# A four-way attention and feed-forward pair in float32: the short key blocks of the causal layer are put together in twos

## The reference, cut to what matters

```
x = x + attn_a(layernorm(x));  x = x + ffn(layernorm(x))
x = x + attn_b(layernorm(x));  x = x + ffn(layernorm(x))      # attn_b: causal

# attn_b, 16 heads of width 8
logits = einsum('bshd,bkhd->bhsk', q, k) / sqrt(8)
logits = where(k_pos > q_pos, -inf, logits)
attn   = softmax(logits, axis=-1)
out    = einsum('bhsk,bkhd->bshd', attn, v) @ W_out + b_out
```

## Time and profile before

| | |
|---|---|
| the profiled execution | 1573.21 us, span 1571.4 us |
| median of 3 runs | 1576.52 us |
| TensorE matmul busy | 1438.6 us, 92% |
| VectorE busy | 1235.9 us, 79% |
| ScalarE busy | 980.0 us, 62% |
| exponentials, L559 | 896, 794.2 us busy |
| job matmuls, L995 | 1792, 657.0 us busy |
| maxima, L785 | 1280, 815.2 us busy |
| weighted sums, L1045 | 3584, 441.6 us busy |
| chain that ended last | PE 70%, DVE 18%, ACT 5%, issue 4% |

### The profile page before, as it was taken

How to read it: one execution, slowest core, us unless ns; L and a number is a source line. 1 busy time by engine, 2 the same in 40 slices (tenths; PEclk the granted TensorE clock), 3 DMA queues, 4 the chain that set the end, 5 groups by cost and what they waited for, 6 DMA issues and landing times.

```text
span 1571.4 us, 26128 instructions
## 1 busy us (share of the span) xinstructions
PE 1438.6 (92%) x9625; PEld 701.7 (45%) x9625; DVE 1235.9 (79%) x3106; ACT 980.0 (62%) x1259; POOL 108.9 (7%) x210
## 2 busy tenths in 40 slices
PE   3699999999999999999988988999999999999888
PEld 2444344434444443444436654444444444444455
DVE  7589999999999998999937757787787877777254
ACT  4427777777777777777774432666666666666622
POOL 6020000000000000000001112000000000000010
PEclk9859999999999999999999985999999999999999
DMA  3720111111101111110001323111121112210000
GB/s 95 221 57 7 27 28 29 29 29 28 28 6 25 28 28 29 28 28 2 2 1 54 83 79 76 35 29 29 29 53 32 29 29 47 38 29 2 8 21 27
DMA packets 40055, 58.39 MB, mean 37 GB/s; under 512 B 7796, under 2 KB 19448, under 8 KB 39928
## 3 DMA queue, kind: packets, MB, share of 16 engines
q1 hardware_dynamic: 39928, 56.72, 15.2%
HBM read 36.77 MB, written 18.87 MB: 35 GB/s over the span
## 4 chain that ended last, share of the span: by engine, by line
PE 70%; DVE 18%; ACT 5%; issue 4%; DMA 2%; SPq 1%; POOL 0%; DVEq 0%; ACTq 0%; POOLq 0%
PE psum L995 25%; PE psum L1045 23%; DVE maxima L785 11%; PE psum L1009 6%; PE psum L1142 5%; PE psum L938 4%; ACT probs L559 3%; DVE junk L782 3%; PE psum L1147 2%; PE psum L1017 1%; PE psum L948 1%; DVE xn L706 1%; PE psum L1062 1%; DMA k_parts<-parts 1%; DMA qop<-shift_rows 1%
## 5 line engine op out<-in xcount | busy, mean ns | idle before, releaser
L559 ACT ACTIVATE probs<-psum 128x1024 f32<-128x1024 f32 (+3 forms) x896 | 794.2, 932 | 300.4 <-PE psum L1009 192.7
L785 DVE TENSOR_REDUCE maxima<-psum 128x1 f32<-128x512 f32 x1280 | 815.2, 684 | 72.8 <-PE psum L995 67.8
L995 PE MATMUL psum<-kop,qop 62*128 62x512 f32 (+3 forms) x1792 | 657.0, 465 | 56.5 <-DVE maxima L782 20.0
L1009 PE MATMUL psum<-qop,kop 64*128 64x512 f32 (+3 forms) x1792 | 498.2, 411 | 10.4 <-ACT probs L559 7.8
L995 PEld LDWEIGHTS psum<-kop,qop 62*128 62x128 f32 x1792 | 289.6, 191 | 487.6 <-DVE maxima L785 325.4
L1045 PE MATMUL psum<-probs,vwin 128*32 128x512 f32 (+3 forms) x3584 | 441.6, 565 | 3.9 <-ACT probs L559 2.0
L782 DVE CUSTOM_DVE_ANT_0 junk<-psum,mask 128x384 bf16<-128x384 f32 (+3 forms) x512 | 237.4, 487 | 75.3 <-PE psum L995 69.8
L1009 PEld LDWEIGHTS psum<-qop,kop 64*128 64x128 f32 x1792 | 242.0, 189 | 55.7 <-ACT probs L559 44.7
L1045 PEld LDWEIGHTS psum<-probs,vwin 128*32 128x32 f32 x3584 | 71.8, 109 | 105.5 <-issue 84.6
L1017 PE MATMUL psum<-half_ident,key_mask 64*128 64x64 bf16 x1024 | 92.7, 198 | 0.0
L1142 PE MATMUL psum<-ffn_xt,wffn 128*128 128x512 f32 x192 | 87.6, 594 | 0.0
(11 more groups left out here) (88 smaller groups left out, 709.9 us busy)
## 6 DMA issues: line engine op xcount, KB each, us to landing
qop<-q_parts SPq DMA_DIRECT2D x256, 64.0 KB
q_parts<-parts SPq DMA_DIRECT2D x32, 256.0 KB, 3.0
k_parts<-parts SPq DMA_DIRECT2D x32, 256.0 KB, 3.4
kop<-k_parts SPq DMA_DIRECT2D x64, 128.0 KB
kop<-k_parts SPq DMA_DIRECT2D x128, 64.0 KB
x<-in_L_attn_a_x SPq DMA_DIRECT2D x8, 256.0 KB, 4.4
qop<-shift_rows SPq DMA_DIRECT2D x128, 8.0 KB
out_x<-x SPq DMA_DIRECT2D x8, 256.0 KB, 2.3
```

The costliest lines, as they stand in the source:

```text
L559: nc.scalar.activation(probs[:, slot, :, c0:], psum[:, bank:bank + 2, c0:], ACT.Exp, scale=SCORE_SCALE).then_inc(probs_ready, 1)
L785: nc.vector.tensor_reduce(dst, src, AX_X, ALU.max).then_inc(ring_free, 1)
L995: mm(psum[:, slot, 0:width], qop[rows, buf, f, r, qb * P:(qb + 1) * P].bitcast(F32R), kop[rows, buf, r, kh * CHUNK:kh * CHUNK + width].bit ...
L1009: ins = mm(psum[:, bank + h, c0:], kop[rows, buf, pair, j * P:(j + 1) * P].bitcast(F32R), qop[rows, buf, f, pair, c0:].bitcast(F32R), star ...
```

## The change

In the causal layer a step may now hold two key blocks. Half 0 has the steps (block 0), (block 2), (blocks 1 and 3); half 1 has blocks 0 to 4 alone, then (block 6), then (blocks 5 and 7). The 384 columns of block 1 or 5 and the 128 of block 3 or 7 lie side by side in one bank: the first block of a step takes the upper columns, the second those below it. Such a unit has 2 + 4 matmuls for each block, one exponential of 2 x 512 columns, and the weighted sums of both blocks stand one behind the other. The matmuls and their columns are the same as before. A window has 10 steps in place of 12, 20 exponentials in place of 24. The plan gives the 48 jobs to 9 steps in place of 11, and the last `project_at` of the layer is 7 in place of 8. The first layer's steps are what they were.

```diff
-            for j in ([0, 3, 2, 1] if causal and f == 0 else range(KB)):
-                c0 = max(0, j * P - f * CHUNK) if causal else 0
-                if c0 < CHUNK:
-                    self.steps.append((f, j, c0))
+            if causal:
+                blocks = [(j,) for j in range(TPC * f)] + [(TPC * f,), (TPC * f + 2,), (TPC * f + 1, TPC * f + 3)]
+            else:
+                blocks = [(j,) for j in range(KB)]
+            for block in blocks:
+
+                pieces, end = [], CHUNK
+                for j in block:
+                    c0 = max(0, j * P - f * CHUNK) if causal else 0
+                    end -= CHUNK - c0
+                    pieces.append((j, c0, end))
+                self.steps.append((f, pieces, end))
...
-PLANS = [..., Plan(causal=True, turn=2, cut=None, idle_steps=1, lead=12, project_at=(2, 4, 8))]
+PLANS = [..., Plan(causal=True, turn=2, cut=None, idle_steps=1, lead=12, project_at=(2, 4, 7))]
...
-                    f, j, c0 = plan.steps[s]
+                    f, _, low = plan.steps[s]
...
-                    nc.scalar.activation(probs[:, slot, :, c0:], psum[:, bank:bank + 2, c0:], ACT.Exp,
+                    nc.scalar.activation(probs[:, slot, :, low:], psum[:, bank:bank + 2, low:], ACT.Exp,
...
+                    for j, c0, low in pieces:
+                        diagonal, high = plan.causal and j * P >= f * CHUNK, low + CHUNK - c0
+                        for h in range(2):
+                            rows = slice(TILE_ROWS * h, TILE_ROWS * h + SCORE_ROWS)
+                            ins = mm(psum[:, bank + h, low:high], kop[rows, buf, pair, j * P:(j + 1) * P].bitcast(F32R),
+                                     qop[rows, buf, f, pair, c0:].bitcast(F32R),
+                                     start=True, stop=not diagonal)
+                        if diagonal:
+                            for part in range(2):
+                                at = low + TILE_ROWS * part
...
+                    for j, c0, low in pieces:
+                        for c in range(HG):
...
+                            ins = mm(psum[32 * c:32 * c + 32, 7, c0:], vwin[:, buf, at:at + 32], probs[:, slot, c % 2, low:low + CHUNK - c0],
+                                     start=(j == 0), stop=(s == plan.half_end[f] and j == pieces[-1][0]), tile_position=(0, 32 * c))
```

More of the change, by code:

```diff
@@ L146, in ends_half @@
         return (c, qb, kh) == (HG - 1, TPC - 1, 0 if self.causal and f == 0 else 1)
-PLANS = [Plan(causal=False, turn=3, cut=32 + 22, idle_steps=0, lead=7, project_at=(6, 8, 11)), Plan(causal=True, turn=2, cut=None, idle_steps=1, lead=12, project_at=(2, 4, 8))]
+PLANS = [Plan(causal=False, turn=3, cut=32 + 22, idle_steps=0, lead=7, project_at=(6, 8, 11)), Plan(causal=True, turn=2, cut=None, idle_steps=1, lead=12, project_at=(2, 4, 7))]
 def transformer_pair_kernel(nc, x_in, wqkv_a, bqkv_a, wout_a, bout_a, wqkv_b, bqkv_b, wout_b, bout_b,
@@ L998, in scores @@
                 def scores(w, buf, s, pair, unit, static_unit):
-                    f, j, c0 = plan.steps[s]
+                    f, pieces, _ = plan.steps[s]
                     bank = 2 * (static_unit % 2)
@@ L1005, in scores @@
                     wait(pe, probs_ready, unit - 1)
[L1006 to L1018, removed]
+                    for j, c0, low in pieces:
[8 more added lines that the diff above has]
+                                at = low + TILE_ROWS * part
+                                for h in range(2):
+                                    rows = slice(TILE_ROWS * h, TILE_ROWS * (h + 1))
+                                    ins = mm(psum[:, bank + h, at:at + TILE_ROWS], key_mask[rows, part, :], half_ident[rows],
+                                             start=False, stop=part == 1)
                     ins.then_inc(scores_ready, 1)
@@ L1041, in weighted_sums @@
                     pe.wait_ge(probs_ready, unit + 2)
[L1042 to L1046, removed]
+                    for j, c0, low in pieces:
+                        for c in range(HG):
+                            slot = (buf * 2 * plan.n + 2 * s + c // 2) % PROBS
+                            at = (j * HG + c) * VH
+                            ins = mm(psum[32 * c:32 * c + 32, 7, c0:], vwin[:, buf, at:at + 32], probs[:, slot, c % 2, low:low + CHUNK - c0],
+                                     start=(j == 0), stop=(s == plan.half_end[f] and j == pieces[-1][0]), tile_position=(0, 32 * c))
                     ins.then_inc(sums_done, 1)
```

## The result

The change made the kernel slower by 0.9%: over 13 runs of each its median was 1594.85 us (1578.25 to 1606.32) against 1573.07 us, and the ratio is 1.0094, with a 95% interval of 1.0058 to 1.0131. The ratio leaves out the two longest runs of the changed kernel, as slow ones. The medians lie further apart, by 1.4%, since its 13 runs form two groups, six from 1578 to 1583 us and seven from 1595 to 1606 us. The profiled execution is the longest of them, so its clock stands for the bad end of the range, and no trace of the lower group was kept; the lengths of its turns at full clock don't depend on that.

The account below looks back on a forecast made before the run. VectorE was taken to pace the first six steps of a turn, TensorE the rest. 15 x (0.28 + 0.40) + 0.8 = 11.0 us off 1573.2 us gave 1562 us, range 1548 to 1577.

Parts of the forecast that it names:

- The clock: Whole kernel: named only as possibly differing between executions, granted 0.98 in these turns against 1.00 in the one cut up.
- VectorE's half: First six steps of a turn, 18.40 us, VectorE pacing: five steps, 32 jobs for 33, 0.40 us less.
- TensorE's lead: In the first three steps of a turn, TensorE is 0.4 us ahead in units and sums.
- TensorE's half: Turn from 1220.20 on, TensorE pacing: 13.05 us against 13.33, 0.28 less; bounds 0.58 less, 0.02 more.
- The step of block 4: First step of TensorE's half: 0.88 + 0.99 + 5 x 0.20 = 2.87 us.
- Merged sums: Weighted sums of 384 and 128 columns in a merged step: 1.07 us, bounds 0.99 and 1.14.
- The last step's wait: A turn's last step: 0.38 us wait for an exponential gets covered; step takes 2.63 us, before 2.82.
- The last turn: Turn without jobs, 25.0 us, chain of exponentials and TensorE: 0.8 us less; bounds 1.8 less, 0.6 more.
- rival (d): Half 1's shift DMA late: at most 0.35 us a turn, up to 1 in the last; 1568 us, chance 0.05.
- (c): VectorE late at the turn's end, L1027 waits 0.6 us: 14 us more, 1587 us; chance 0.08.
- (a): Nothing gained in the causal turns: they stay at 31.7 us, about 1573 us (1568 to 1578); chance 0.22.

Follow-up runs that it names:

- the filler: Changed kernel with three bf16 matmuls of 512 columns, result overwritten, ahead of a turn's fourth job: 1576.30 us, ratio 1.0019 to the kernel before.
- Half 1 alone: Kernel before with only blocks 5 and 7 of half 1 sharing a step: 1560.64 us, ratio 0.9922.
- 3, 4, 3: Changed kernel with the ten jobs of a turn's first step standing 3, 4, 3 where they stood 5, 3, 2: 1588.19 us, ratio 1.009.
- in phase: Changed kernel, jobs dealt: 3, 4, 3 in the first step, 21 instead of 20 through after the third: 1576.19 us, ratio 1.0015.
- Half 0 alone: Kernel before with only blocks 1 and 3 of half 0 sharing a step: 1604.51 us, ratio 1.0196.

## Why the prediction was wrong

**The clock, a term that the sum put at nothing.** The prediction held everything but the steps constant and named the clock only as something that might differ between executions. It differs between the kernels, and that is most of the loss: about 11.8 us of 14.8 by the ratios. The hint was in the trace: the one turn in the kernel before that lasted 34.19 us at a clock of 0.90 has its low stretch from 1107.5 to 1114.5, in the same place as nearly every turn of the changed kernel, right after the wait of 0.58 us and the 128-column jobs. The change puts its five smallest jobs and a longer wait exactly there. The Trainium skill's page TensorE: Matmul & The Clock Gate, Part 1, says that activity is what releases the lower clock; the filler agrees, with ten of twelve turns below full clock in the profile without it and none in the one with it.

**VectorE's half: the step of the sum that failed.** The prediction took 0.40 us off it; it became 0.37 us longer. That turns a turn that should be 0.68 us shorter into one that is 0.18 longer. It had followed the first three steps (VectorE 0.2 us later at job 22, TensorE 0.4 ahead). At the end of the third the kernel after ended the norm of half 0 11.52 us after the start, as before (11.55), so TensorE's lead never came: the five jobs first cost 0.21 us, shown both ways. The rest of the half was assumed to run as before but for one job less, worth 0.61 us. It didn't: the shift by one job turned the ring's content around, and VectorE idled 0.44 us more at the three runs of sums. The job less was worth 0.05 us, shown both ways too. I counted jobs in each half and not which of them stand in front of the sums.

**TensorE's half was right in direction and within its bounds.** Predicted 0.28 us less, measured 0.19 less; 13.05 us with 16 jobs, measured 13.21. The step of block 4, with five jobs, took 3.18 and not 2.87 us, since VectorE came late into it. Half 1 alone, with 15 jobs, took 12.72 us. Merged sums took 1.00 us (1417.00 to 1418.00, start to start), at the lower bound of 0.99 to 1.14. That agrees with the rule of the Trainium skill's page TensorEngine Tiling (Array Packing), Key Properties, that changing the tiling mode, not just the tile, drains the array; no run separates this from other costs of starting a run. The last step's wait of 0.38 us for the exponential went, as predicted.

**The last turn** got 0.54 us shorter from the shift copy to the activation table load (24.91 to 24.37 us), where I had said 0.8. In it the shift DMA is waited for, 0.59 us where rival (d) had said up to 1:

```profile
1491.74 0.83 PE L1017 MATMUL psum<-qop,kop 64*128 64x512 f32 x4 [0.59 <-DMA qop<-shift_rows]
```

The copy ended at 1489.13, so the rows land after about 2.6 us; in the profile's complete turns with jobs no unit waits for them.

**The rivals.** (c), the slower one, named the wrong place: VectorE late at the turn's end. In the causal turns L1035 (L1027 before) never waited for GpSimd; VectorE is late in the middle. That its 1587 us comes near the measured time is luck. (a) was nearest for the work, since full-clock turns changed by 0.18 us only, but through a loss and a gain that nearly cancel: 0.69 gained by half 1's merge, and more than that lost by half 0's. The forecast of 0.68 us a turn and 11 us in all is, by chance of the same size, what half 1 alone gives: 0.69 us and 11.2 us.

**What stays open.** The clock also falls with 3, 4, 3 jobs and a wait of only 0.31 us, and in phase in five turns of twelve. It is shown that the turn's first steps do it in most turns and that more matmul work there cures it in the changed kernel; which of short matmuls, short waits and the merged unit counts for how much is not settled, and neither is why some executions of the changed kernel lose far less than others. Half 0 alone loses 0.98 us a turn at full clock: its VectorE's half is as long as in the full change, 18.69 us, and TensorE's, 14.00 us, is 0.60 longer than before, 0.50 of it in the step of block 4 with its fifth job. Five jobs first and the phase account for 0.65 of the 0.98; the rest is open.

## What to carry to other kernels

When a plan deals out work in proportion, a change of the steps moves every job behind it: before predicting, print the new order, and look at what each ring or buffer holds at the moment when its producer turns away for a microsecond. Try the parts of a change alone, since here one gave 11 us and the other took more. And read a clock below full in a single turn of the kernel before as a warning: here it marked the stretch in which waits and short matmuls then cost TensorE half its clock for 7 us in most turns.

## What the runs showed that I had not expected

- The clock fell to 0.50 within a few microseconds of light work, with no standstill of TensorE longer than 0.83 us, and stayed there for 6.8 us (1219.0 to 1225.8), or for stretches of 3.4 us in the kernels with 3, 4, 3 and some others. Each long stretch costs about 2.4 us: 34.26 against 31.90.
- Three matmuls whose result nobody reads, some 0.65 us in each of 15 turns, took the loss from 0.94% to 0.19%, about 11.8 us.
- A merge of two weighted sums, 16 matmuls of 384 and 128 columns, costs what one of 512 columns does: 1.00 us against 0.99.
